# Chaining the four groups of small products that make attention's outputs, through a semaphore that TensorE raises for itself

## The chip, the cores and the metric

The kernel runs on one core of one Trainium2 chip. The metric is the device time of one execution in microseconds (us); the kernel before was run three times, and its median is the number that the prediction is set against. The engines are named as the profile names them: PE is TensorE's products, PEld its weight loads (both are one engine, and weight loads run beside products), DVE is VectorE, ACT is ScalarE, POOL is GpSimd, SP is SyncE. Every product on TensorE is a weight load followed by a matmul. A float32 product runs in two passes, so that one call of `matmul` in the program leaves two weight loads and two matmuls in the trace.

## What is computed

The reference takes an input of 8 batches, 1024 tokens and 256 channels through a model of two parts, an attention model and a feed-forward one. The attention model has two grouped convolutions with a layer norm, then four layers of linear attention, then a feed-forward block. One layer of linear attention, for each batch, is

```python
q = gelu(x @ Wq + bq) + 0.21
k = gelu(x @ Wk + bk) + 0.21
v = x @ Wv + bv
q_r, k_r = rope(q), rope(k)
z = 1.0 / (einsum(q, mean(k)) + 1e-06)
kv = einsum('bhnd,bhne->bhde', k_r, v) / n
out = einsum('bhnd,bhde->bhne', q_r, kv) * z
return layernorm(out + x, g, bb)
```

with 16 heads of 16 channels. The change touches only the einsum that makes `out` from the rotated queries and `kv`.

## The kernel before

The program has three stages that follow one another on the clock: the convolutions (up to about 150 us), attention (about 150 to 985 us) and, after some 75 us of preparation, the two feed-forward blocks (to the end at 1828 us).

**Units.** `attention_phase` works through 32 units (`UNITS = B * L`, 8 batches by 4 layers). Four batches are in work at a time (`LANES = 4`), so that a unit never needs the result of the unit just ahead of it. Each engine has its program written out by hand, a loop over the units, and the engines are tied together by counting semaphores alone. TensorE's loop for unit n is, in this order: the products of keys and values of unit n-1 (`key_value`, line 903), transposes of the second half of the tokens (`turn_u`, line 846), four key projections (`project`, through `mm3`, lines 32 to 34), one product that turns `kv` of unit n-1 (`turn_kv`, line 916), eight transposes of keys (`turn_k`, line 866), the outputs of unit n-1 (`outputs`, line 934), eight more transposes of keys, the query projections, the values, the transposes for the next unit, and the denominators (line 888). After the last unit `key_value`, `turn_kv` and `outputs` stand by themselves, followed by the next stage.

**The outputs.** `outputs` takes the 256 channels as two blocks of 128 (`db`). For each block it multiplies the cosine half of the rotated queries (`qc`) by `kv`, and then the sine half (`qs`) by `kv_rot`, and adds the two up in the same PSUM banks. Both weights are block diagonal, so that each of these four steps is cut into 16 small products of 32 by 32 weights and 256 moving columns (written 32*32 and 32x256 in the profile): `i` picks one of four 32-row strips of TensorE's array and the bank (`big[i]`), `j` one of four 32-column strips. The 16 products of a step therefore lie on 16 different tiles of the array; the next step uses the same 16 tiles again in the same order. In what follows these four steps are groups one to four: (`db` 0, `qc`), (`db` 0, `qs`), (`db` 1, `qc`), (`db` 1, `qs`). A block is the whole of `outputs` for one unit: 64 products, 128 weight loads and 128 matmuls in the trace. Ahead of the block TensorE waits for the rotated queries (`s_qr`, `s_qd`), for `kv_rot` (`s_kvr`, a copy on DVE at line 1160) and for the banks (`s_lo`); inside the block nothing waits, and the last product of it raises `s_out`.

**Who waits for the outputs.** DVE transposes the result (line 1105) after `s_out`, scales it by z (line 1112) and adds the residual (line 1118). POOL's rotation of the next unit's queries into `qc` and `qs` (`rotate_q`, lines 800 and 801) may start only after `s_out` as well.

**Waits in the program.** All waits of the attention program go through the class `Waits` (line 26), which leaves out a wait whose value has already been waited for. One semaphore wait rides on the next instruction; further ones ahead of the same instruction become instructions of their own.

Of the kernel before, what the change touches and what calls it, by code (L numbers as in the profile page):

```python
# [611 lines left out]
def attention_phase(nc, u_in, u_out, T, H, w_split, bias_qk, bias_v, keep, place, sems, stack, d_u0, d_u4, prefetch,  # L612
# [3 lines left out]
    TILES = T // P  # L616
    DUOS = TILES // 2
    CB = H // P
# [6 lines left out]
    GR = 4  # L625
    D = P // GR
# [4 lines left out]
    QUARTERS = P // D  # L631

    ctx = ExitStack()
    with ctx:
        sb = lambda n, s, d=F32: stack.enter_context(nc.sbuf_tensor(n, s, d))
        pb = lambda n, s: ctx.enter_context(nc.psum_tensor(n, s, F32))
        sem = lambda n: sems.enter_context(nc.semaphore("att_" + n))

        y_rows = [place[f"yB{s}"] for s in range(LANES)]
        kr, qc, qs, gT, v, gain, shift, rot, kv_mask, mean_mask = (  # L640
            place[n] for n in ("kr", "qc", "qs", "gT", "v", "gain", "shift", "rot", "kv_mask", "mean_mask"))
# [11 lines left out]
        kv = sb("kv", [P, CB, D])  # L653
        kv_rot = sb("kv_rot", [P, CB, D])
# [12 lines left out]
        big = [pb(f"big{i}", [P, 512]) for i in range(GR)]  # L667
# [7 lines left out]
        s_q, s_gelu, s_gq, s_qr, s_qd, s_v, s_vs = (sem(n) for n in ("q", "gelu", "gq", "qr", "qd", "v", "vs"))  # L675
        s_ksum, s_km, s_den, s_dens, s_dent, s_z = (sem(n) for n in ("ksum", "km", "den", "dens", "dent", "z"))
        s_kv, s_kvm, s_kvw, s_rot, s_kvr = (sem(n) for n in ("kv", "kvm", "kvw", "rot", "kvr"))
        s_out, s_turned, s_scaled, s_y = (sem(n) for n in ("out", "turned", "scaled", "y"))
        s_stats, s_mom, s_var, s_rstd, s_off, s_unit = (sem(n) for n in ("stats", "mom", "var", "rstd", "off", "unit"))


# [9 lines left out]
        quarter = lambda q, j: q.rearrange("p (a c) -> p a c", a=TILES)[:, :, D * j:D * j + D]  # L691
# [136 lines left out]
        def tensor(e, then):  # L828
            w = Waits(e)
# [89 lines left out]
            def outputs(n):  # L919
                w.wait_ge(s_qr, 3 * n + 3)  # L920
                w.wait_ge(s_qd, n + 1)
                w.wait_ge(s_kvr, n + 1)
                if n + 1 < UNITS:
                    w.wait_ge(s_lo, 4 * (n + 1) + 4)
                else:
                    w.wait_ge(s_vs, 4 * n + 4)

                for db in range(CB):
                    for wt, q in ((kv, qc), (kv_rot, qs)):
                        for j in range(QUARTERS):  # L930
                            for i in range(GR):
                                ch = slice(D * i, D * i + D)
                                out = big[i][D * j:D * j + D, :].rearrange("p (a d c) -> p a d c", a=TILES, d=CB)[:, :, db, :]
                                m = e.matmul(out, wt[ch, db, :], quarter(q[ch, db, :], j), start=q is qc, stop=q is qs)  # L934
                m.then_inc(s_out, 1)

            conv.tensor(e, lambda: turn_u(0, 0), lambda: turn_u(0, 1))
            for n in range(UNITS):
                if n >= 1:
                    key_value(n - 1)  # L940
                    turn_u(n, 1)
                project(n, 0, "k", 0)
                project(n, 0, "k", 1)
                project(n, 1, "k", 0)
                project(n, 1, "k", 1)
                if n >= 1:
                    turn_kv(n - 1)
                turn_k(n, 0)
                turn_k(n, 1)
                if n >= 1:  # L950
                    outputs(n - 1)
                turn_k(n, 2)
                turn_k(n, 3)
                for x in range(QH):
                    for db in range(CB):
                        project(n, x, "q", db)
                for u in range(DUOS):
                    values(n, u)
                if n + 1 < UNITS:
                    turn_u(n + 1, 0)  # L960
                denominators(n)
            key_value(UNITS - 1)
            turn_kv(UNITS - 1)
            outputs(UNITS - 1)
            then(e, lambda: None)

# [922 lines left out]
def build(nc, t):  # L1889
# [5 lines left out]
    with ExitStack() as ctx:  # L1895
# [64 lines left out]
        def prefetch(e, pairs):  # L1960
# [3 lines left out]
            for j in pairs:  # L1964
                for half in range(2):
# [3 lines left out]
        conv = conv_phase(nc, t["x_conv"], t["bands1"], t["bands2"], t["bias1"], t["bias2"], t["eye"], t["u0"], comp, t["tri"],  # L1969
                          w_col, picks, prep, keep, place, ctx, layers, d_u0, load_tables, load_tables_q)  # L1970
        attention = attention_phase(nc, t["u0"], t["u4"], T, H, t["w_split"], bias_qk, bias_v, keep, place, ctx, layers, d_u0,
                                    d_u4, prefetch, conv)
        layers.close()
# [128 lines left out]
```

## Time and profile before

| | |
|---|---|
| median of 3 runs | 1833.14 us (1832.21 to 1834.62) |
| profiled execution, its own time | 1829.56 us |
| its span on the core | 1827.8 us |
| granted TensorE clock, mean | 0.998 of full speed |
| busy: PE / PEld | 99% / 81% |
| busy: DVE / ACT / POOL | 80% / 51% / 56% |
| chain that ended last: PE's share | 96% |
| matmuls of line 934, in the whole run | 4096 (2048 on `qc`, 2048 on `qs`) |

The profile describes one execution; its span lies 1.8 us under its own time, and that time 3.6 us under the median of the runs. "Busy" is the share of the span in which an engine had at least one instruction in flight. Several matmuls can be in flight at once, so that a busy PE says nothing of how densely they follow each other; where they follow how closely has to be read from their starts. The end of a matmul is modelled by the profiler.

### The profile page before, as it was taken

To read this page: it belongs to the slowest core of one execution; us is meant where nothing else is said; L and a number is where in the kernel's file an instruction comes from. 1 tells how busy PE (TensorE), PEld (TensorE's weight loads), DVE (VectorE), ACT (ScalarE), POOL (GpSimd) and SP (SyncE) were. 2 spreads that over 40 slices of the span, in tenths; PEclk is the share of its full clock that TensorE was granted. 3 is DMA by queue.
4 is the path that set the end of the run, shared out by engine and by line. 5 is a ranking of instruction groups with operands and counts; after the bars stand their busy time and mean duration, and the time that the engine had idled before them with its cause. 6 is when DMAs were issued, how large, how long until landed. Compare 5 with 4: busy or idle time off the path is not lost.

```text
span 1827.8 us, 46210 instructions
## 1 busy us (share of the span) xinstructions
PE 1806.2 (99%) x19196; PEld 1477.8 (81%) x19196; DVE 1455.7 (80%) x3454; ACT 936.8 (51%) x1741; POOL 1016.6 (56%) x775
## 2 busy tenths in 40 slices
PE   9999999999999999999999999999999999999998
PEld 3336888888888888888887988888888888888887
DVE  3667787888888888888888768888888888888887
ACT  5554776677667776677667742222322232323231
POOL 1557998999999999999985012222222222222221
PEclk9999999999999999999999999999999999999999
DMA  8372210100103210000105931010101010101000
GB/s 294 150 268 111 94 60 3 37 2 2 37 2 106 94 37 3 29 10 3 60 3 197 306 101 35 36 35 29 42 24 47 24 47 24 46 24 44 26 12 24
DMA packets 25234, 115.38 MB, mean 63 GB/s; under 512 B 4480, under 2 KB 5440, under 8 KB 19904
## 3 DMA queue, kind: packets, MB, share of 16 engines
q1 hardware_dynamic: 21104, 89.69, 14.0%
q0 software_dynamic: 1152, 12.58, 2.0%
q10 hardware_dynamic: 2768, 10.15, 1.5%
q8 instruction: 151, 2.47, 0.6%
q14 instruction: 59, 0.48, 0.1%
HBM read 80.95 MB, written 31.46 MB: 62 GB/s over the span
## 4 chain that ended last, share of the span: by engine, by line
PE 96%; DVE 2%; ACT 1%; DMA 1%; issue 1%; POOL 0%; ACTq 0%; SPq 0%; DVEq 0%; POOLq 0%
PE bankC L1450 13%; PE bankC L32 7%; PE bankC L33 7%; PE bankC L34 7%; PE ring L32 6%; PE ring L34 6%; PE ring L33 6%; PE bankC L1449 6%; PE big L934 5%; PE big L34 3%; PE big L33 3%; PE big L32 3%; PE ring L866 3%; PE big L846 3%; PE conv_ps L256 3%; PE hid_ps L245 3%
## 5 line engine op out<-in xcount | busy, mean ns | idle before, releaser
L1450 PE MATMUL bankC<-down,act_hi 128*128 128x512 f32 x992 | 353.1, 397 | 0.0
L1449 PE MATMUL bankC<-down,act_lo 128*128 128x256 f32 x868 | 246.2, 284 | 0.0
L1450 PEld LDWEIGHTS bankC<-down,act_hi 128*128 128x128 f32 x992 | 186.3, 188 | 41.9
L1575 DVE TENSOR_TENSOR act_lo<-gel,act_hi 128x512 fp32r<-128x512 f32 x256 | 210.5, 822 | 8.7
L33 PE MATMUL bankC<-aT_lo,up_hi 128*128 128x512 f32 x512 | 199.6, 390 | 0.0
L32 PE MATMUL bankC<-aT_hi,up_hi 128*128 128x512 f32 x512 | 199.5, 390 | 0.0
L34 PE MATMUL bankC<-aT_hi,up_lo 128*128 128x512 f32 x512 | 199.4, 389 | 0.0
L1529 POOL TENSOR_TENSOR hC<-hC,vecC 128x1024 f32<-128x1024 f32 x16 | 38.7, 2416 | 282.9 <-PE turn L1424 282.9
L1535 POOL TENSOR_TENSOR rstdC<-var_epsC,minus_halfC 128x4 f32<-128x4 f32 x47 | 56.1, 1193 | 249.5 <-DVE var_epsC L1603 249.5
L1449 PEld LDWEIGHTS bankC<-down,act_lo 128*128 128x128 f32 x868 | 164.1, 189 | 1.4
L774 POOL TENSOR_TENSOR kr<-kr,kc 128x512 f32<-128x512 f32 x128 | 161.9, 1299 | 0.0
L1492 ACT ACTIVATE aT_hi<-turn 128x512 fp32r<-128x512 f32 x64 | 34.8, 596 | 234.8 <-PE turn L1424 234.8
L1500 ACT ACTIVATE gel<-bankC,b1s 128x512 f32<-128x512 f32 x128 | 88.4, 690 | 128.8 <-PE bankC L34 112.6
L793 POOL TENSOR_TENSOR yB<-yB,shift 128x1024 f32<-128x1024 f32 x64 | 151.3, 2389 | 0.0
L1500 ACT ACTIVATE gel<-bankC 128x512 f32<-128x512 f32 x128 | 76.8, 600 | 141.8 <-PE bankC L34 125.0
L790 POOL TENSOR_TENSOR yB<-yB,gain 128x1024 f32<-128x1024 f32 x48 | 114.8, 2412 | 43.3 <-PE big L846 43.2
L1074 DVE TENSOR_TENSOR hT_lo<-big,hT_hi 128x512 fp32r<-128x512 f32 x128 | 82.3, 685 | 62.7 <-ACT hT_hi L973 62.5
L1013 ACT ACTIVATE yB<-yB,offset,rstdB 128x256 f32<-128x256 f32 x256 | 129.5, 587 | 0.0
L982 ACT ACTIVATE gkT<-ring,bias_qk 128x512 f32<-128x512 f32 x128 | 88.3, 690 | 79.6 <-PE ring L34 79.6
L801 POOL TENSOR_TENSOR qs<-gT,sin_q 128x512 f32<-128x512 f32 x96 | 124.6, 1298 | 0.0
L800 POOL TENSOR_TENSOR qc<-gT,cos_q 128x512 f32<-128x512 f32 x96 | 124.5, 1297 | 0.0
L1564 DVE TENSOR_TENSOR aT_lo<-turn,aT_hi 128x512 fp32r<-128x512 f32 x64 | 41.1, 684 | 104.7 <-ACT aT_hi L1492 104.7
(215 smaller groups left out, 5262.3 us busy)
## 6 DMA issues: line engine op xcount, KB each, us to landing
raw_late<-in_AB SPq DMA_DIRECT2D x30, 320.0 KB, 4.0
u<-hA SPq DMA_DIRECT2D x8, 1024.0 KB, 5.0
u_next<-u SPq DMA_DIRECT2D x8, 1024.0 KB, 6.0
hC<-u SPq DMA_DIRECT2D x16, 512.0 KB, 4.0
xC<-in_x SPq DMA_DIRECT2D x16, 512.0 KB, 4.8
out<-w_flat SPq DMA_DIRECT2D x15, 512.0 KB, 2.6
w_flat<-in_AB SPq DMA_DIRECT2D x22, 320.0 KB, 3.7
w_split<-w_parts ACTq DMA_DIRECT2D x4, 1536.0 KB, 5.9
```

What stands on the lines that cost most here:

```text
L32: e.matmul(out, wh, xh, start=start, stop=False)
L33: e.matmul(out, wh, xl, start=False, stop=False)
L34: return e.matmul(out, wl, xh, start=False, stop=stop)
L774: e.tensor_tensor(kr[:, u, :], kr[:, u, :], kc[:, u, :], ALU.add).then_inc(s_kr, 1)
L793: e.tensor_tensor(tiles(y, a), tiles(y, a), row(shift), ALU.add).then_inc(s_res, 1)
L800: e.tensor_tensor(qc[:, db, cols], gT[:, db, cols], table_q(cos_q, db, x), ALU.mult)
L801: e.tensor_tensor(qs[:, db, cols], gT[:, db, cols], table_q(sin_q, db, x), ALU.mult).then_inc(s_qr, 1)
L1013: e.activation(y[:, o, :], y[:, o, :], ACT.Identity, bias=offset[:, two, o:o + 1], scale=rstd[:, two, o:o + 1]).then_inc(s_unit, 1)
L1449: e.matmul(bank[:, 0:H], a_lo[:, fb, tok], both[k][:, fb, 0, :], start=False, stop=False)
L1450: m = e.matmul(bank[:, :], a_hi[:, fb, tok], both[k][:, fb, :, :].rearrange("p a h -> p (a h)"), start=fb == 0, stop=fb == FB - 1)
L1500: e.activation(gel[:, n % GEL, :], bank_of(i, k, s, fb)[:, :], ACT.Gelu if k == 0 else ACT.Gelu_apprx_tanh, bias=b1s[:, fb:fb + 1] if k == ...
L1575: e.tensor_tensor(a_lo[:, fb, :], g, a_hi[:, fb, :].bitcast(F32), ALU.subtract).then_inc(s_act_lo, 1)
```

## The change

`outputs` gets a semaphore of its own, `s_tile`. The first product of groups one, two and three (`i` 0, `j` 0) raises it when it is done, and the first product of groups two, three and four waits for that: group g+1 is issued only once the first product of group g is done. The number, the order and the operands of the products stay as they are. The first product of a group had no wait of its own before, so the new one rides on that product's first weight load, and the program has as many instructions as before.

```diff
-        s_out, s_turned, s_scaled, s_y = (sem(n) for n in ("out", "turned", "scaled", "y"))
+        s_out, s_turned, s_scaled, s_y, s_tile = (sem(n) for n in ("out", "turned", "scaled", "y", "tile"))
...
-                for db in range(CB):
-                    for wt, q in ((kv, qc), (kv_rot, qs)):
-                        for j in range(QUARTERS):
-                            for i in range(GR):
-                                ch = slice(D * i, D * i + D)
-                                out = big[i][D * j:D * j + D, :].rearrange("p (a d c) -> p a d c", a=TILES, d=CB)[:, :, db, :]
-                                m = e.matmul(out, wt[ch, db, :], quarter(q[ch, db, :], j), start=q is qc, stop=q is qs)
+                for g, (db, wt, q) in enumerate((db, wt, q) for db in range(CB) for wt, q in ((kv, qc), (kv_rot, qs))):
+                    if g:
+                        w.wait_ge(s_tile, 3 * n + g)
+                    for j in range(QUARTERS):
+                        for i in range(GR):
+                            ch = slice(D * i, D * i + D)
+                            out = big[i][D * j:D * j + D, :].rearrange("p (a d c) -> p a d c", a=TILES, d=CB)[:, :, db, :]
+                            m = e.matmul(out, wt[ch, db, :], quarter(q[ch, db, :], j), start=q is qc, stop=q is qs)
+                            if g < 3 and i == 0 and j == 0:
+                                m.then_inc(s_tile, 1)
                 m.then_inc(s_out, 1)
```

On TensorE the block of one unit stands as follows, the same in all 32 units (`x16` is 16 instructions in a row that read alike; `32x8x32` is the 256 moving columns).

```order
-L934 MATMUL big<-qc,kv 32x8x32 [waits att_kvr,att_qr]
-L934 MATMUL big<-qc,kv 32x8x32 x15
-L934 MATMUL big<-qs,kv_rot 32x8x32 x16
-L934 MATMUL big<-qc,kv 32x8x32 x16
-L934 MATMUL big<-qs,kv_rot 32x8x32 x16
+L935 MATMUL big<-qc,kv 32x8x32 [waits att_kvr,att_qr]
+L935 MATMUL big<-qc,kv 32x8x32 x15
+L935 MATMUL big<-qs,kv_rot 32x8x32 [waits att_tile]
+L935 MATMUL big<-qs,kv_rot 32x8x32 x15
+L935 MATMUL big<-qc,kv 32x8x32 [waits att_tile]
+L935 MATMUL big<-qc,kv 32x8x32 x15
```

Nothing changes its place; a wait stands at the first product of group two and at that of group three, and the fourth group has one in the same way.

## Rows read from the trace of the kernel before

**Rows 1.** The page: span, busy time by engine, the chain's shares by engine

```profile
span 1827.8 us, 46210 instructions
...
PE 1806.2 (99%) x19196; PEld 1477.8 (81%) x19196; DVE 1455.7 (80%) x3454; ACT 936.8 (51%) x1741; POOL 1016.6 (56%) x775
...
PE 96%; DVE 2%; ACT 1%; DMA 1%; issue 1%; POOL 0%; ACTq 0%; SPq 0%; DVEq 0%; POOLq 0%
```

**Rows 2.** Stretches of one unit each, busy us (instructions) by engine, clock, DMA

```profile
212.84:238.42 25.58, 25.58 (x403) 22.04 (x403) 21.57 (x51) 18.02 (x38) 25.50 (x18) 1.00 0.24 84
700.00:725.57 25.57, 25.57 (x403) 22.04 (x402) 21.59 (x51) 18.01 (x38) 23.80 (x17) 1.00 0.01 2
```

**Rows 3.** The chain that ended last, 211.6 to 216 us: start, us, what

```profile
211.64 0.23 PE ring L34
211.86 0.17 PE big L916 x2
212.03 0.88 PE ring L866 x8
212.91 2.69 PE big L934 x118
215.60 0.48 PE ring L866 x3
```

**Rows 4.** Timeline, weight loads, five narrow stretches: start, us, engine, line, what

```profile
187.27 0.23 PEld L934 LDWEIGHTS big<-qc,kv 32*32 32x32 f32 x32 [0.17 <-issue]
187.51 0.10 PEld L934 LDWEIGHTS big<-qs,kv_rot 32*32 32x32 f32 x1
...
187.92 0.10 PEld L934 LDWEIGHTS big<-qs,kv_rot 32*32 32x32 f32 x1
...
188.56 0.10 PEld L934 LDWEIGHTS big<-qc,kv 32*32 32x32 f32 x1
...
189.21 0.12 PEld L934 LDWEIGHTS big<-qs,kv_rot 32*32 32x32 f32 x2
```

**Rows 5.** Timeline, matmuls: group one's second passes, the last product, what follows

```profile
187.51 0.47 PE L934 MATMUL big<-qc,kv 32*32 32x256 f32 x16
187.73 0.37 PE L934 MATMUL big<-qs,kv_rot 32*32 32x256 f32 x1
...
189.66 0.37 PE L934 MATMUL big<-qs,kv_rot 32*32 32x256 f32 x1
189.96 0.33 PE L866 MATMUL ring<-identity,gkT 128*128 128x128 f32 x1
```

**Rows 6.** Stretches, line 934 alone: us, PE busy (in flight), PEld busy (in flight), clock, DMA

```profile
187.62:187.73 0.11, 0.11 (x33) 0.00 (x0) 1.00 0.00 0
187.74:187.91 0.17, 0.17 (x22) 0.10 (x1) 1.00 0.00 0
187.92:188.17 0.25, 0.25 (x29) 0.25 (x30) 1.00 0.00 0
```

**Rows 7.** Timeline after the last unit: a weight load and a block that wait for DVE

```profile
981.11 0.41 DVE L1153 SCALAR_TENSOR_TENSOR kv<-bias_v,kr_sum,ring 128x32 f32<-128x32 f32 x2
981.57 0.30 PEld L916 LDWEIGHTS big<-kv,rot 128*128 128x128 f32 x2 [1.56 <-DVE kv L1153]
...
982.05 0.22 DVE L1160 COPY kv_rot<-big 128x64 f32<-128x64 f32 x1 [0.53 <-PE big L916]
...
982.39 0.27 PEld L934 LDWEIGHTS big<-qc,kv 32*32 32x32 f32 x32 [0.52 <-issue]
```

**Rows 8.** Who waited, TensorE; then the block of 289.58 and its neighbour, line 934 alone

```profile
PE big L934 <- issue: 5.0, 8, 1.1
...
187.27:189.66 2.39, 2.39 (x128) 1.81 (x128) 1.00 0.03 7
289.58:293.12 3.54, 2.92 (x128) 1.86 (x128) 1.00 0.02 5
```

**Rows 9.** Timeline, matmuls 292.2 to 293; instruction fetches 289.6 to 290.1, 290.1 to 291.6

```profile
291.83 0.39 PE L934 MATMUL big<-qs,kv_rot 32*32 32x256 f32 x2
292.84 0.44 PE L934 MATMUL big<-qs,kv_rot 32*32 32x256 f32 x7 [0.62 <-issue]
...
DMA packets 0, 0.00 MB, mean 0 GB/s; under 512 B 0, under 2 KB 0, under 8 KB 0
...
q8 instruction: 1, 0.02, 5.5%
```

**Rows 10.** Transposes of keys ahead of the block, ns min/median/max; DVE after the block

```profile
186.30 0.93 PE L866 MATMUL ring<-identity,gkT 128*128 128x128 f32 x7
...
L866 PE MATMUL ring<-identity,gkT x512: 271/273/329, 163.2 to 966.4; 128*128 128x128 f32 x171
...
190.07 0.73 DVE L1105 STREAM_TRANSPOSE big<-big 128x512 f32<-128x512 f32 x1 [0.57 <-PE big L934]
```

## The prediction

> **What bounds the kernel now.** The page comes first: PE is busy 99% of a span of 1827.8 us and holds 96% of the chain that ended last [rows 1]. That is an average, so the attention stage is looked at by itself. Two units, 212.84 to 238.42 and 700.00 to 725.57, each take 25.57 to 25.58 us, and TensorE is busy in all of it; DVE has 4 us to spare [rows 2]. POOL is at 25.50 us in one and 23.80 in the other with the same length, so it doesn't set it. The chain goes from product to product through the block of outputs, with no other engine between [rows 3]. So a nanosecond more or less per block comes out at the end, 32 times.
>
> Inside a block "busy" says nothing, so I read starts. From the first weight load of group one (187.27) to the start of the last matmul (189.66) it takes 2.38 us [rows 4, 5]. Group one runs as 16 tiles should: its 32 weight loads cover 0.23 us, so their starts lie within 0.13, about 8 ns per product [rows 4]. Its second passes begin at 187.51, 0.24 later [rows 5]. Then comes a **hold**. One weight load of group two is taken ahead at 187.51, and its matmul starts at 187.73, when tile 0 is free [rows 4, 5]; but from 187.62 to 187.73 no weight load is in flight, from 187.74 to 187.91 a single one [rows 6], and the second product begins at 187.92 [rows 4]. The other 15 tiles had nothing to load, though a new product could have followed on each 0.22 after its last pass, as on tile 0. Two more such holds end at 188.56 and 189.21, 0.65 apart [rows 4].
>
> What ends a hold? A second pass takes 0.37 us, so group one's first product (187.51) is done at 187.88 or 187.89 [rows 5]; product 18 of the block begins 0.03 after that. My reading: TensorE keeps only some 17 products in hand, and a further one comes in when the oldest is **done**, not when it was issued. They then come in at 30 weight loads in 0.25 us, two per product: one product per 17 ns [rows 6], half the pace of group one, which had lined up behind the transposes [rows 10].
>
> **The change, step by step, for one block.**
>
> 1. *Instructions.* None is added, and none moved. Three products raise a semaphore and three wait.
>
> 2. *Price of one release.* No row shows TensorE waiting for itself. The nearest is a weight load that had truly waited, for DVE: DVE ends at 981.11 + 0.41 = 981.52, the load starts at 981.57, so 0.05 us [rows 7]. I take that. Upper end: a block that waited for `kv_rot`, whose copy ended at 982.27, began at 982.39, 0.12 later [rows 7]; that start had an instruction for a wait of its own ahead of it, which the change doesn't have. Lower end: 0.04, as DVE starts on the outputs at 190.07 [rows 10] when their last product ended at 189.66 + 0.37 = 190.03 [rows 5]; that would make the three waits 0.03 cheaper together.
>
> 3. *One group to the next.* Second pass 0.24 after the group's first load, done 0.37 after that, release 0.05: 0.66, unrounded nearer 0.67. Groups start at 0, 0.67, 1.34, 2.01. The old distance was 0.65. So the first product of group two starts at 187.94 instead of 187.73, but that tile's head start was worth little: the other 15 went at 187.92 and go at 187.94. The wait takes the place of the hold, almost to the same instant.
>
> 4. *Within a group.* The collision that made the hold is gone, but if the reading above is right the products behind the waiting one still come in only as old ones are done, from 0.03 before the release, 17 ns apart. The last of 15 loads at 2.01 - 0.03 + 15 x 0.017 = 2.23 or 2.24, its second pass follows 0.24 later: 2.47. Against 2.38 that is +0.09, and less with the rounding in my favour; I take **+0.08 us per block**. Lower end: the group lines up complete behind the wait and goes at 8 ns per product as group one did: 2.01 + 0.13 + 0.24 = 2.38, and 2.35 with group one's own 0.34 from first load to last matmul. That is -0.03 per block. Upper end, below among the rivals.
>
> 5. *What follows the block.* The transposes start 0.30 after the block's last matmul began [rows 5]; that stays. DVE's first transpose of the outputs comes 0.08 later and has slack [rows 2]. Nothing queued behind the block waits for more than TensorE itself.
>
> 6. *Where it is hidden.* In 8 of the 32 blocks TensorE ran out of instructions: 5.0 us of it as idle time [rows 8]. The block at 289.58 takes 3.54 us instead of 2.39 [rows 8]: its matmuls stop at 291.83 and go on at 292.84 [rows 9]. An instruction fetch lies in it, none running in 289.6 to 290.1, one beginning just after 290.1 and taking 5.5% of 16 x 1.5 = 1.3 us [rows 9]. The end of such a stall hangs on the fetch, which began before group two's 15 products did, so it swallows the +0.08. If that cover failed, the eight would add 8 x 0.08 = 0.6 us.
>
> The sum: 24 x 0.08 = **+1.9 us**, with nothing from the other eight. 1829.56 becomes 1831.5 in a profiled execution; the median of the runs lies 3.6 above that one, 1833.14, and becomes **1835.1**. Bounds of step 4: 32 x -0.03 = -1.0 us. A change of 0.2% (3.7 us), about what a measurement of this kernel tells from none, isn't reached by any of these.
>
> **A rule that speaks against the change.** Of the eight transposes ahead of a block the fourth raises a semaphore, and yet seven of them in a row, with that one among them, lie in 0.93 us: at 0.27 each they start 0.11 apart [rows 10], which leaves no room for a gap. So I book nothing for the three raises. The Trainium skill, in "TensorE: Matmul & The Clock Gate", section on the cost of the per-tile semaphore tail, has every raise by packed tiles cost about 26 ns, one after the other, and advises a single one on the last tile. By it 96 raises would add about 2.5 us, an estimate from that page; no run here has raises inside a packed group, so it stays a rival.
>
> **The rivals.**
>
> *A. The wait also stops the supply (slower).* If the products behind a waiting weight load aren't taken in while it waits, each group restarts from nothing. The price per wait is then the upper release of step 2, 0.12 for 0.05, so 3 x 0.07 = 0.21 a block, plus 0.03 for the supply that no longer runs ahead: 0.08 + 0.24 = +0.32. It decides from +0.12 per block on 32 blocks. Total 24 to 32 times 0.32: +7.7 to +10 us, 1841 to 1843. Against it: group one of the last block began right after its wait, and yet its 32 loads cover 0.27 us [rows 7], 10 to 11 ns per product, so 16 products stood ready behind that wait. 12%.
>
> *B. Raises cost something inside a packed group (slower).* If each holds the tile's queue for as long as two products come in, 2 x 17 ns [rows 6], that is 3 x 0.034 = 0.10 per block, +3.3 us over 32, and +5.2 with the sum: 1838.3. For it: nothing in the rows; against it, the transposes, which fill the whole array and not a tile. It is the rule just named, priced from rows. 8%.
>
> *C. The stalls for instructions shrink (faster).* Each of the eight costs about a microsecond: 3.54 - 2.39 = 1.15 in the one shown, at most 8 x 1.15 = 9 us. If the new pacing has TensorE take instructions in later, the fetch is in time more often. To pass 0.2% the change must save 5.6 us against my sum. Against it: pacing by completion is what step 4 finds before as well. Four of the eight gone: 1835.1 - 4.6 = 1830.5; all: 1826. 8%.
>
> *D. Groups go complete behind the wait* (lower end of step 4): -1.0 us, 1832.1. 20%. For it, the last block's group one; against it, the 17 ns after every hold.
>
> *The change does nothing* would need the wait to be met always; it can't be, since a group's first product isn't done before 0.61 and group two's load stood ready at 0.24.
>
> **How the numbers follow.** My forecast 52%, A 12%, B 8%, C 8%, D 20%. The predicted time is the likeliest case's. Forecast and D end within 0.2% (1829.5 to 1836.8), except for the error of two medians, whose runs spread by 2.4 us; for that I move 4% from them to faster and 2% to slower. Faster: 6% of C and the 4%, 0.10. Slower: A, B and the 2%, 0.22. Same: the rest, 0.68. The range goes from 1830.5 (D less its spread, the milder C) to 1841 (B, and A's near end): it leaves out the rest of A and of C, about 15%.
>
> **What would show it.** Right: loads of group two start together at 0.67 after group one's first, groups 0.67 apart, last matmul at 2.46 to 2.47, a unit 25.65 us instead of 25.57, the same eight stalls ending as long after their fetch. For D: 16 products within 0.13 in every group and 2.35. For A: groups 0.74 or more apart. For B: a gap behind each raising product. Wrong altogether: a block under 2.3 us without a stall, which would mean that a product's end frees something earlier than I read, or stalls in more or fewer blocks.

## The result and the profile after

The changed kernel takes 1836.43 us, the median of 20 runs, against 1833.53 for the kernel before, also of 20 runs: a ratio of 1.0018, 95% interval 1.0011 to 1.0025. That is 2.9 us between the medians, 2.0 to 4.6 by the interval. The forecast was +1.9 us and 1835.1, in a range of 1830.5 to 1841: the time lies inside the range, and the +1.9 just under the interval.

The page of the changed kernel, its span and engines, against [rows 1]:

```profile
span 1834.4 us, 46210 instructions
...
PE 1812.2 (99%) x19196; PEld 1463.6 (80%) x19196; DVE 1455.5 (79%) x3454; ACT 936.8 (51%) x1741; POOL 1016.5 (55%) x775
...
PE 96%; DVE 2%; DMA 1%; ACT 1%; issue 1%; POOL 0%; ACTq 0%; SPq 0%; DVEq 0%; POOLq 0%
```

As many instructions, the same chain. The two profiled executions lie 6.6 us apart, more than the medians; where the surplus is comes below. The units first, in the same two places as [rows 2] (columns: stretch, us, then busy us and instructions of PE, PEld, DVE, ACT, POOL, clock, DMA):

```profile
212.56:238.25 25.69, 25.69 (x405) 21.57 (x403) 21.58 (x51) 18.02 (x39) 25.61 (x18) 1.00 0.25 84
705.58:731.26 25.68, 25.68 (x405) 21.56 (x403) 21.57 (x51) 18.01 (x39) 23.78 (x17) 1.00 0.01 2
```

A unit is 0.11 us longer, and no other engine moved. The block of one unit, weight loads in narrow stretches of the timeline, against [rows 4] (start, us, engine, what, idle time before and its releaser):

```profile
212.83 0.13 PEld L935 LDWEIGHTS big<-qc,kv 32*32 32x32 f32 x6 [0.17 <-issue]
...
213.50 0.10 PEld L935 LDWEIGHTS big<-qs,kv_rot 32*32 32x32 f32 x1 [0.44 <-PE big L935]
...
214.17 0.10 PEld L935 LDWEIGHTS big<-qc,kv 32*32 32x32 f32 x1 [0.31 <-PE big L935]
...
214.84 0.10 PEld L935 LDWEIGHTS big<-qs,kv_rot 32*32 32x32 f32 x1 [0.30 <-PE big L935]
```

Groups start at 0, 0.67, 1.34 and 2.01, to the hundredth what step 3 said. The trace now names the releaser, TensorE itself, where the hold before had none. Then the block's last matmul and what follows it, against [rows 5], and the stretches of line 935 alone, against [rows 6]:

```profile
215.32 0.37 PE L935 MATMUL big<-qs,kv_rot 32*32 32x256 f32 x1
215.62 0.33 PE L866 MATMUL ring<-identity,gkT 128*128 128x128 f32 x1
```

```profile
213.21:213.49 0.28, 0.28 (x32) 0.00 (x0) 1.00 0.00 0
213.51:213.76 0.25, 0.25 (x24) 0.25 (x31) 1.00 0.00 0
212.83:215.33 2.50, 2.50 (x128) 1.33 (x128) 1.00 0.03 7
```

From first load to last matmul 2.49 us instead of 2.38: **+0.107 us per block** (2.489 and 2.382 from the first to the last matmul start, within 2 ns in all blocks that no fetch stalls, except the last block of the kernel before, 2.371). The prediction had 0.08 and worked it out as 2.47. Before the release not a single load is in flight in 0.28 us; behind it they come in at one product per 17 ns, not 7.

### The profile page after: what moved, and what is told of

It reads as the page before. It is cut to its first block, busy times and chain, and to the rows that moved or that the text cites. A ratio compares the mean times of both kernels' runs of the same rounds, so it can differ in the third digit from the quotient of the medians.

```text
span 1834.4 us, 46210 instructions
## 1 busy us (share of the span) xinstructions
PE 1812.2 (99%) x19196; PEld 1463.6 (80%) x19196; DVE 1455.5 (79%) x3454; ACT 936.8 (51%) x1741; POOL 1016.5 (55%) x775
## 3 DMA queue, kind: packets, MB, share of 16 engines
q8 instruction: 151, 2.47, 0.6%
## 4 chain that ended last, share of the span: by engine, by line
PE 96%; DVE 2%; DMA 1%; ACT 1%; issue 1%; POOL 0%; ACTq 0%; SPq 0%; DVEq 0%; POOLq 0%
PE bankC L1453 13%; PE bankC L32 7%; PE bankC L33 7%; PE bankC L34 7%; PE ring L32 6%; PE ring L34 6%; PE ring L33 6%; PE bankC L1452 6%; PE big L935 5%; PE big L34 3%; PE big L33 3%; PE big L32 3%; PE ring L866 3%; PE big L846 3%; PE conv_ps L256 3%; PE hid_ps L245 3%
## 5 line engine op out<-in xcount | busy, mean ns | idle before, releaser
L32 PE MATMUL bankC<-aT_hi,up_hi 128*128 128x512 f32 x512 | 199.5, 390 | 0.0
```

The source lines that it names most:

```text
L32: e.matmul(out, wh, xh, start=start, stop=False)
```

## The experiments

Each time is set against the kernel before on the same chip; the edits are to the changed kernel, except for the half groups and the kernels called "before". Blocks are measured from the first to the last matmul start; the number given is that of the blocks without a fetch stall.

### Raises without waits

```diff
-                    if g:
-                        w.wait_ge(s_tile, 3 * n + g)
```

> The three raises of the semaphore stay, the three waits for it go. My reading (a further product is taken in only when the oldest in hand is done, and a raise costs nothing): block as in the kernel before, 2.38 us from the first to the last matmul start where no instruction fetch stalls it, time within 0.1% of the kernel before. Rival (a raise by a product in a packed group costs some 26 to 34 ns): block 2.46 to 2.48, and most of the change's +0.107 per block is explained by raises.

1834.29 us, ratio 1.0006 (0.9997 to 1.0016). The block takes 2.41 us, 0.027 more than without raises. The loads of this block (first one at 214.66):

```profile
215.33 0.10 PEld L933 LDWEIGHTS big<-qs,kv_rot 32*32 32x32 f32 x1
...
215.98 0.10 PEld L933 LDWEIGHTS big<-qc,kv 32*32 32x32 f32 x1
...
216.63 0.10 PEld L933 LDWEIGHTS big<-qs,kv_rot 32*32 32x32 f32 x1
```

The first hold ends 0.67 after the block's start instead of 0.65; the others are again 0.65 apart. So one of the three raises costs about 27 ns and the other two nothing, and neither expectation came out. By the starts, the holds end with products 18, 35 and 52 of the block, 17 apart, so they wait for the ends of products 1, 18 and 35; the raises are on products 1, 17 and 33, and only the first of these is one that a hold waits for. That the hold's end moves by as much as one product's end is put off also speaks for the reading itself. A raise isn't free, then, but raises alone don't explain the change.

### Every product raises

```diff
-                            if g < 3 and i == 0 and j == 0:
+                            if (g, i, j) != (3, GR - 1, QUARTERS - 1):
                                 m.then_inc(s_tile, 1)
```

and the waits are gone as in the experiment before.

> No waits, but every product of the block raises the semaphore, 63 instead of 3. If a raise costs nothing: block 2.38 us as in the kernel before. If raises of products on different tiles come one after the other at about 26 ns each: the first products are done 26 ns apart instead of 7 to 17, which holds back what is taken in behind them, block above 63 x 26 ns = 1.6 us plus the 0.6 of the first product to be done, and the time at least 0.2% up; a price of 20 ns or more would show as a block over 2.5 us.

1844.44 us, ratio 1.0067 (1.0050 to 1.0084), block 2.87 us. Line 933 alone (us, matmuls in flight, loads in flight):

```profile
213.87:214.43 0.56, 0.56 (x31) 0.56 (x27) 1.00 0.00 0
213.19:216.07 2.88, 2.87 (x128) 2.53 (x128) 1.00 0.03 6
```

27 loads, thirteen or fourteen products, in 0.56 us: by their starts one product per 43 ns where [rows 6] had 17. A raise adds 26 ns to the time in which one product follows another out of TensorE's hands. By the Trainium skill, "TensorE: Matmul & The Clock Gate", section on the cost of the per-tile semaphore tail, raises by packed tiles come one after the other at 26.3 ns each. This run agrees within a nanosecond (42.5 less 16.7 by the starts). Of the expectation, the rival with a price of 26 ns came out, not the free raise.

### Half groups, no semaphore

```diff
-                for db in range(CB):
+                for db, pair in ((db, pair) for db in range(CB) for pair in (0, 2)):
                     for wt, q in ((kv, qc), (kv_rot, qs)):
-                        for j in range(QUARTERS):
+                        for j in (pair, pair + 1):
```

> No semaphore; the block is walked in halves: 8 tiles with the first weights, the same 8 tiles with the second, then the other 8 tiles. Every ninth product now finds its tile busy while only 8 are in hand. Reading A (what holds is that 17 products are in hand and the oldest is not done): no weight load waits for an end; each pair of passes takes its 0.43 to 0.46 us on the tile, 8 half groups one after the other, block about 3.5 us. Reading B (a product that meets a busy tile makes the next one wait until that tile's last pass is done, 0.4 us after it started): 0.65 per half group, block about 5.0 us.

1842.53 us in one run, block 2.68 us: neither number. The 3.5 of reading A was a mistake in working it out, since the third half group lies on tiles other than the first two and needs not wait for them. What counts is when its products are loaded (block from 214.96):

```profile
215.39 0.10 PEld L934 LDWEIGHTS big<-qc,kv 32*32 32x32 f32 x1
...
215.58:215.60 0.02, 0.02 (x16) 0.00 (x0) 1.00 0.00 0
...
215.61 0.10 PEld L934 LDWEIGHTS big<-qc,kv 32*32 32x32 f32 x1
```

The 17th product and the 18th both go to tiles that have been idle since the block began. The 17th is loaded at 0.43, behind the eight that wait for their tiles; the 18th not before 0.65, with nothing being loaded just ahead of it. That is the moment at which the block's first product is done and the hold ended in the kernel before. So an idle tile doesn't avoid the hold: reading A stands, with a wrong block time, and reading B's 5.0 us is out.

### Waiting for the last product instead of the first

```diff
-                            if g < 3 and i == 0 and j == 0:
+                            if g < 3 and i == GR - 1 and j == QUARTERS - 1:
                                 m.then_inc(s_tile, 1)
```

> As the change, but each group waits for the LAST product of the group ahead, not the first. Reading A (products are taken in behind the waiting one as the oldest ones get done, 17 ns apart, from 0.65 us after the group began): at the release some 0.3 us later than now nearly the whole group stands ready and goes at about 7 ns per product (its 16 first passes within 0.10 to 0.12 us); groups 0.77 us apart, block 3 x 0.77 + 0.34 = 2.65 us. Reading B (nothing is taken in behind a waiting load): the 16 first passes of every later group spread over 0.25 us, groups 0.77, 0.92 and 0.92 apart, block 3.1 us.

1853.17 us in one run, block 3.12 us. Two releases, and the stretches behind them (block from 213.60):

```profile
214.53 0.10 PEld L935 LDWEIGHTS big<-qs,kv_rot 32*32 32x32 f32 x1 [0.69 <-PE big L935]
...
215.45 0.10 PEld L935 LDWEIGHTS big<-qc,kv 32*32 32x32 f32 x1 [0.68 <-PE big L935]
```

```profile
214.52:214.64 0.12, 0.11 (x15) 0.11 (x28) 1.00 0.00 0
215.44:215.56 0.12, 0.11 (x15) 0.11 (x27) 1.00 0.00 0
```

Fourteen products' worth of loads in 0.12 us: the group did line up behind the wait, as A said, and B said 0.25. But the releases are 0.92 apart, the first one 0.15 later than A's 0.77. Both facts fit one statement (the profile's ends of matmuls are modelled and can't show it directly): products *leave* TensorE's hands at one per 17 ns even when they were issued at one per 7 ns. The sixteenth of a group that went in within 0.10 us is therefore done 15 x 0.017 = 0.25 after the first, 0.15 later than it was issued behind it. The 17 ns of [rows 6] are the pace of ending, not of supply; the block of 3.12 came out as reading B expected it, for A's reason.

### Waiting with the second product

```diff
-                    if g:
-                        w.wait_ge(s_tile, 3 * n + g)
...
+                            if g and i == 1 and j == 0:
+                                w.wait_ge(s_tile, 3 * n + g)
```

> As the change, but the wait rides on the second product of the group, not the first. The second product of groups two to four had to wait until the first one of the group ahead had been done anyway. If the change's cost per block is one raise that holds up the hold's end (0.03) and 2 x 0.04 because the first product of groups three and four starts only after the release: here the first product keeps its early start, the second is released where the hold ended, and the block takes 2.41 to 2.43 us instead of 2.49. If the wait costs by itself, wherever it stands: 2.49 us.

1837.59 us in one run, which tells little: besides the nine blocks that stall for instructions in the other kernels with raises, the block at 318 and the last one stall in it. The block without a stall takes 2.41 us:

```profile
214.52:216.93 2.41, 2.41 (x127) 1.83 (x128) 1.00 0.03 7
```

In the block, the same three raises and waits now cost the one raise and nothing else. The wait's price in the change is the place where it stands, ahead of the one product that could start early.

### The same block at another place of the program

The trace of before stalls for instructions in 8 blocks. Counted off in the traces, TensorE's instruction after every such stall inside a block has place 193 modulo 256, in the kernel before and in the changed one. The queue of these fetches has 151 of them, of 16384 bytes each, for the 38717 instructions that the trace has on TensorE: 256 to a fetch, 64 bytes each. A unit has 810 or 811 instructions, so the seam, the end of one fetched piece, wanders through the blocks. To move it, waits for values long reached were added to the projections and values (two of them make one instruction):

```diff
+            def pad(sem_, value, count):
+                for _ in range(count):
+                    e.wait_ge(sem_, value)
...
                 w.wait_ge(s_lo, 4 * n + 2 * x + 2)
+                pad(s_lo, 4 * n + 2 * x + 2, 14 + (0 if (n, x, kind, db) == (0, 1, "q", 1) else 0))
...
                 w.wait_ge(s_lo, 4 * n + 4)
+                pad(s_lo, 4 * n + 4, 14 + (0 if u else 2 - (n % LANES == LANES - 1)))
```

This was done to the kernel before (`p_before` in the texts below) and to the changed one (`p_after`); the third kernel (`p_bad`) is `p_before` with 120 instead of the 0 in the first `pad`, which moves all later blocks by 60 instructions.

> The kernel before, with 85 further instructions per unit on TensorE that only wait for a value long reached, spread over the projections and values, so that a block of outputs begins at place 18 to 168 of its 256 instructions of 64 bytes, never at 205 to 10. If the stalls for instructions come from a block that straddles the end of a fetched piece of 256 instructions near its own end: no stall in any block, 8 x 1.0 = 8 us less, about 1825 us (-0.45%), every block 2.38 us. If they come from elsewhere, or the further instructions cost time: 8 stalls still there, 1833 us or more (85 x 0.05 us x 32 = 136 us at worst if nothing hides them).

> The changed kernel with the same further instructions. With no stalls in either, what the change does to the blocks alone is left: 32 x 0.107 = +3.4 us against p_before, about 1828.5 us, every block 2.49 us. If part of the change's cost lay in additional stalls, the distance between p_after and p_before is no larger than that, and smaller than between the two kernels' own profiles (6.6 us).

> As p_before, with 60 more of the same instructions once, in the first unit, so that every other block begins at place 205 to 228, where the kernel before has its stalls. If the place makes the stalls: 16 or 17 blocks of 3.1 to 3.6 us, the others 2.38, and 16 x 1.0 = 16 us more than p_before (the 60 themselves at most 3 us, once). If the number of instructions cures the stalls in itself: no stall, same time as p_before within 3 us.

Padded before: 1834.29 us, ratio 1.0001 (0.9992 to 1.0010). Padded after: 1836.48, 1.0011 (1.0002 to 1.0020). Put in the bad place: 1851.25, 1.0099 (1.0084 to 1.0114). Who waited on TensorE for instructions, in the padded kernel before, then in the one put in the bad place (us in total, times, longest):

```profile
PE ring L32 <- issue: 3.1, 4, 1.7
...
PEld ring L32 <- issue: 11.1, 17, 2.1
PEld big L940 <- issue: 5.7, 32, 0.5
```

```profile
PE big L940 <- issue: 6.9, 15, 0.8
...
PEld big L940 <- issue: 20.1, 48, 1.3
```

The line of the outputs is gone from PE's list in the first (5.0 us in [rows 8]), where only the last block is still long (3.34 us), and stands with 15 stalls in the second; blocks of 2.38 us stand beside blocks of 3.1 to 3.7 there. So the place of the block in the program makes the stalls. The total of 16 us more, which `p_bad` was to take, came out at 17 in part by luck: the 60 instructions, booked at 3 us at most, put the first block off by 7.5 us, and from the first block to the last it is 9.3 us more. But the 8 us weren't gained in `p_before`: they came back at the first key projection (L32), the place behind the short products of keys and values, where every other unit was 0.1 to 1.3 us longer, and one 2.1:

```profile
187.94:214.59 26.65, 25.83 (x403) 22.11 (x402) 21.57 (x51) 17.72 (x37) 26.49 (x20) 1.00 0.24 81
214.59:240.19 25.60, 25.60 (x404) 22.03 (x403) 21.58 (x51) 18.03 (x38) 25.42 (x18) 1.00 0.23 84
```

Two further paddings were to keep the seam off both places. The first (`q_before`, `q_after`) has 36 waits where 14 stood and 100 more once, and 1024 instructions per unit; the second (`r_before`, `r_after`) none in the first two key projections, 16 in the other projections and 18 in the values, and 896 per unit.

> The kernel before with some 214 further waits' instructions per unit instead of 85, so that a unit has 1024 instructions, four pieces of 256, and every block but the last begins at place 135. In the kernel padded to 895 no block stalled any more, but the end of a piece then fell into the end of the 256 short products of keys and values in every other unit, and stalls of 0.5 to 1.1 us stood behind those. Now it falls 63 instructions into a block of outputs and so well inside the products of keys and values (some 150 instructions in). If the place alone decides: no stall over 0.45 us between two starts on TensorE from 200 to 960 us, every unit 25.57 us, 8 us less: about 1825 us, ratio 0.995 to 0.997. If the fetches simply take their time wherever they fall, or 214 instructions can no longer be hidden (0.05 us each, 11 us of a unit's 25.6): no gain, 1833 us or more.

> The changed kernel with the same further instructions. If the place alone decides, the change costs 31 x 0.107 = 3.3 to 3.4 us against q_before, all in the blocks (2.49 us for 2.38), about 1828.5 us.

> The kernel before with 86 further instructions that only wait, none of them in the two projections right behind the products of keys and values, where the kernel padded to 895 lost 0.1 to 1.1 us in every other unit; the others spread at 8 to 11 per projection or value. A unit has exactly 896 instructions, and blocks begin at places 157 and 29. If place decides and 8 to 11 instructions are hidden as 7 were: no stall, units 25.57 to 25.65 us, 8 us less minus at most 1 to 2: about 1826 to 1828 us, ratio 0.996 to 0.997. If 11 are not hidden (18 were not: 0.8 us of idle time at each): units 26 us or more and 1845 us or more.

> The changed kernel with the same further instructions. With no stall in either, the change's own price is left: 32 x 0.107 = +3.4 us against r_before (0.18%); 0.1 to 0.25% with the error of the runs.

| kernel | median, us | ratio to the kernel before (95%) | block, us | typical unit, us |
|---|---|---|---|---|
| 1024, before | 2084.35 | 1.1362 (1.1346 to 1.1378) | 2.38 | 33.5 |
| 1024, changed | 2091.95 | 1.1414 (1.1398 to 1.1429) | 2.49 | 33.8 |
| 896, before | 1838.96 | 1.0029 (1.0017 to 1.0041) | 2.38 | 25.65 and 26.1, in turn |
| 896, changed | 1842.40 | 1.0052 (1.0038 to 1.0066) | 2.49 | 25.75 and 26.2, in turn |

No block stalls in any of the four, except the last one, but neither padding is a gain: 18 waiting instructions in a row cost about 0.8 us of idle time each time and 250 us in all, and the 896 ones still left every other unit 0.1 to 1.1 us too long, and one of them much more (30.5 us in `r_before`, 28.4 in `r_after`). The expectations had priced such an instruction at 0.05 us, which is its duration in the trace; in a row they start 0.106 us apart, so that 18 take 1.9 us. That fits the 7.5 us of `p_bad`: 67 in a row are 7.1. I found no version that beats the kernel before. What they do give is an estimate of the change's price without stalls in blocks: 1842.40 - 1838.96 = 3.4 us, where 32 x 0.107 = 3.4 had been expected, and 1836.48 - 1834.29 = 2.2 us in the first pair. The 3.4 is a rough agreement and no more: it comes from six and five runs that spread by up to 5.6 us, and in the two profiles the stretch from the first block to the last is equally long (801.3 and 801.4 us), because the one long unit is 2.0 us shorter in `r_after` and other stalls differ too. The pair of 1024 lies 7.6 us apart, and each unit there is 0.3 longer with the block 0.107 longer; where the rest of that comes from I didn't find.

## Why the prediction was right, step by step

**What bounds the kernel** held: a unit grew by what its block grew by, 0.11 us, and DVE and POOL stayed where they were. The block was forecast at +0.08 and grew by 0.107; with that, the sum's 24 blocks make 2.6 us and not 1.9.

**Step 2, the release**, was taken as 0.05 us from rows in which TensorE waited for DVE. It fits a wait for itself as well: 0.24 to the second pass, 0.37 for its end and 0.05 make 0.66, unrounded 0.67, and the groups stand 0.67 apart. The DVE instruction waited for there raises a semaphore too, so this price has a raise in it.

**Step 3, the wait in place of the hold**, held, and the half groups and the wait for the last product show why. TensorE has some 17 of these products in hand at most, and the next comes in as the oldest is done. Whether the wait is there or not, group two can't begin in earnest before 0.65.

**Step 4, the supply**, was right in size and half wrong in its reason. The 17 ns are how fast products end, not how fast new ones are brought up. In the kernel as changed the two can't be told apart, because the wait is only just longer than the hold.

**The term that was mis-sized** is the +0.08 of step 4, and by little: 0.107 measured. Its own sum, 2.01 - 0.03 + 15 x 0.017 + 0.24, is 2.475 against 2.382, which is +0.093; taking +0.08 for it is half of the miss. The other half, 0.016, lies mostly in the lead that the products are given. By the starts, group four's first load is at 2.015, the last product's at 2.249, 0.234 later, and its second pass 0.242 after that, at 2.491: behind the release the products have a lead of 0.015 and not 0.03. "I book nothing for the three raises" rested on transposes that fill the array, and said so. As a statement on raises in a packed group it is wrong; the sum didn't suffer by it, since the release of step 2 holds a raise. Raises without waits move the end of the first hold from 0.646 to 0.673, and with the wait the release is at 0.672.

The experiments divide the 0.107 otherwise: 0.027 for the raises without waits, nothing more for waits on the second product (2.41 again), and 0.08 for waits on the first. This last part is two times 0.04, for groups three and four, and the starts show it. Against the kernel with raises alone, the first matmul of product 18 begins 0.003 later, that of product 35 is 0.040 later, that of product 52 0.082, and the last matmul 0.080. The first product of groups three and four leaves later than it did, and the others follow it. That these 0.08 equal the +0.08 of step 4 is chance: step 4 adds up other terms.

**Step 6, the cover**, held as far as one profile of each kernel can tell. The eight blocks that stalled before stalled again, at 3.26 to 3.83 us against 3.27 to 3.56, with their own pace 0.107 slower, and in the kernel in which every product raises, whose blocks are 0.49 slower, the same eight take 3.27 to 3.58. Together the eight are 0.8 us longer than before, which is also what an uncovered 8 x 0.107 would make. But singly they moved by -0.28 to +0.55 us, and with every product's raise, where 8 x 0.49 = 3.9 us stood to be added, they are again only 0.8 longer. And the fetch's own record settles most of it: TensorE goes on 2.31 to 2.67 us after the fetch in the block began before the change, 2.31 to 2.68 after it. A stalled block's end is the fetch's, not the products'. The times of the runs can't show it: 24 x 0.107 = 2.6 us and 32 x 0.107 = 3.4 lie both within 2.0 to 4.6. The block of 289.87, against [rows 8, 9]:

```profile
289.87:293.15 3.28, 3.04 (x128) 1.39 (x128) 1.00 0.02 5
...
292.85 0.66 PE L935 MATMUL big<-qs,kv_rot 32*32 32x256 f32 x13 [0.24 <-issue]
```

**The surplus of the profile.** From the first load of the first block to that of the last it is 795.1 us before and 800.0 after. Of these 4.9 us, 22 blocks without a stall make 22 x 0.107 = 2.4; a ninth block that stalls (the one at 471.97) 1.0; the eight others 0.8; the short products of keys and values ahead of the last block 0.4; the remaining 0.3 is spread over the other units. A stall in the last block itself adds 1.8 us behind it; that one isn't the change's, since the half groups have it too and the kernel in which every product raises has not. The ninth stall stands in every profile of a kernel whose blocks raise the semaphore without padding (five of them) and in neither of the two that don't, but each of these is one execution, and the seam lies at the edge of what stalls there. Whether the change brings such stalls about is open. The medians don't decide it: 23 x 0.107 and one stall of 1.0 make 3.5 us, and the interval goes to 4.6.

**The rivals.** A, supply stopped by the wait, is out: a group lines up complete behind a long enough wait, and groups aren't 0.74 apart. B was right in kind: a raise costs 26 to 27 ns where something waits for the product's end, where B had 34. Its total, 0.08 + 0.10 = 0.18 per block against 0.107, was too much, because the release of step 2 already has a raise in it. C didn't come about; the stalls stayed or grew. D, groups going at 7 ns behind the wait, was seen only where the wait is 0.25 us longer than here, and there it costs more than it saves.

## What to carry to other kernels

Where many small products go out back to back, look at when the weight loads start, not at the busy share, and set a gap's end against the end of an earlier product (here the one 17 places ahead): holding products back didn't close a gap that ends there. A semaphore wait that "replaces" such a gap cost at least its raise here, and more where it stood ahead of a product that had a head start. Before expecting something of a stretch with hundreds of short instructions, see whether instruction fetches stall it, and remember that any edit that changes the number of instructions ahead of it moves those stalls.

## What the runs showed of the hardware

- Small float32 products (32 by 32 weights, 256 columns) start at 7 ns from each other if they were in hand, and TensorE has 17 of them in hand: in the kernel before, the holds end with products 18, 35 and 52. They are done, as far as holds and releases show it, at no less than 17 ns from each other; with a raise on each it is 43 ns, so 26 ns per raise. Of three raises without waits, only the one on a product whose end a hold waits for showed in the time.
- An instruction fetch of 256 instructions kept up with TensorE except where nearly all 256 are short: a whole block of outputs in 2.4 us, or the products of keys and values. TensorE went on 2.3 to 2.7 us after such a fetch had begun; a stalled block was 0.7 to 1.4 us longer than one without a stall (kernel before, changed, and put in the bad place; 1.5 and 1.7 in the last blocks of the latter two).
- Instructions that only wait start 106 ns apart on TensorE, though each is recorded as 51 ns long. Seven, put in front of a projection of 1.4 us, cost nothing or little; 18 cost 0.8 us each time.
